# Moving GpSimd's side jobs around the state recurrences of a two-layer kernel

## The chip, the cores and the metric

The program runs on one core of one Trainium2 chip. Its time is the device time of one execution in microseconds (us). Each version is run several times on the same chip and the median is given. TensorE is PE in the rows, VectorE is DVE, ScalarE is ACT, GpSimd is POOL, and SP is the engine that issues most of the DMAs.

## The reference

Two pre-norm layers work on x, of 2 batches x 1024 rows x 128 features. The first has attention with 16 heads and a routed feed-forward part. The second has a selective state-space mixer and a dense mixture of eight experts. The change touches only the second layer:

```python
# mixer, for each batch; d_inner 256, d_state 16
h   = x @ fc1_w.T + fc1_b
...
hstate = dA * hstate + (dt_t * u_t)[..., None] * B_t[:, None, :]   # for each of 1024 steps
y_t    = jnp.einsum('bdn,bn->bd', hstate, C_t)
...
out = y @ out_proj_w.T
x   = x + out @ fc2_w.T + fc2_b
# dense experts, E = 8, hidden 256 each: every row goes through all of them
h = gelu(einsum('nd,edh->neh', xf, w1) + b1)
y = einsum('neh,ehd->ned', h, w2) + b2
x = x + (y * norm_g[:, None, None]).sum(axis=1)
```

## The kernel before

One Python list of steps, `K.order`, is walked once per engine. Each engine has a table from step names to functions (`POOL_STEPS` for GpSimd) and issues the instructions of those steps that it has, in the order of the list. So the place of a step in the list is its place in each engine's queue, and the queues run in order: an instruction that waits on a semaphore holds back all that stand behind it on its engine. `first_inputs_order`, `recurrence_order` and `dense_order` write the three parts of the list that matter here.

**Recurrences.** There are 2 batches x 2 halves of d_inner x 16 states = 64 units, `("unit", u)`, each over 1024 time steps. For each unit TensorE spreads a row of B over the partitions (L936), ScalarE forms the decay dA (L1387), VectorE multiplies the gain (L1923) and runs the scan (L1930), GpSimd multiplies the states by C (`hc`, L2252), and TensorE adds that product to Y (L952). The states and products have three buffers each. The dictionary `one` says which other steps stand behind which unit. Among them is `("fc2bias", b)`: GpSimd adds the bias fc2_b to batch b of x in place (L2230), once the normalised rows have been made from x. VectorE needs it later, in `dve_fc2`.

**Dense experts.** Full precision is got from three reduced-precision matmuls: high x high, high x low, low x high. ScalarE casts the weights to the high part (`w1hi`, `w2hi`), and GpSimd subtracts it from the weights to get the low part: `w1lo` e (L2260) and `w2lo` e (L2267), a 128x256 piece for each of the eight experts. TensorE's up products (`up1`, L1029) need `w1lo`; its down products (`down1`, L1046) need `w2lo`. There are 4 x 16 of each, numbered n; number n of the first 16 belongs to expert n // 2. The first 14 up products run behind units 49 to 62 and ScalarE parks their results (`pre`). ScalarE's gelu follows, its cast of the hidden part to high (L1471) and VectorE's subtraction for the low (`split1`, L2028: `e_hr_lo<-e_h,e_hr_hi`). Those hidden parts have four buffers. Down product n - 3 stands at step n of the dense list.

Two waits matter. The down products wait so:

```python
    if n < M1 and m % (F1 // P) == 0:
        pe.wait_ge(Y.w2_split, m // (F1 // P) + 1)
```

And `pre` number 11 overwrites the first layer's weight buffer that holds w1, so ScalarE first waits there until all eight `w1lo` are done (`Y.w1_split`, 8).

Beside the down products, the dense list has the layer norm of the second batch and the gate of the first. At step 11 stands `("lnvar", 7), ("lnroot", 7)`: VectorE's moments, then GpSimd's root (L2102, L2105). At step 12 stands `("e1_lg", 0), ("e1_root", 0)`: VectorE's gate sums (their last instruction L1960), then GpSimd's root of them (L2151).

Of the kernel before, what the change touches and what calls it, by code (L numbers as in the profile page):

```python
# [43 lines left out]
E1, F1 = 8, 256  # L44
# [17 lines left out]

PRE_EW = 11

LAST_ROWS, LAST_BANK = (B - 1, SEQ // CH - 1), B * (SEQ // CH) * M1 - 1


# [125 lines left out]
def turned(n):  # L193

    return [("lnturn", n, 0), ("lnturn", n, 1), ("lncopy", n, 0), ("lncopy", n, 1)]
# [158 lines left out]
def first_inputs_order():  # L354


    s = NSLOT
    order = turned(4) + [("down", s + 4), ("fc1", 0), ("fc1_out", 0), ("yrow", s + 4), ("fetch", s + 10)]
    order += [("down", s + 5), ("up", s + 6), ("gelu", s + 6), ("inp", 0, 0), ("inp_out", 0, 0), ("yrow", s + 5), ("fetch", s + 11)]
    order += [("inp", 0, 1), ("inp_out", 0, 1), ("up", s + 7), ("gelu", s + 7), ("down", s + 6)]  # L360
    for i in range(4):
        order += [("conv", 0, i // 2, w) for w in (i % 2 * 2, i % 2 * 2 + 1)]
        order += [("yrow", s + 6 + i)] + [("fetch", s + 12 + i)] * (i < 3) + ([("up", s + 8 + i), ("gelu", s + 8 + i), ("down", s + 7 + i)] if i < 3 else [])
    order += [("silu", 0, 0), ("up", s + 11), ("down", s + 10), ("silu", 0, 1), ("up", s + 12), ("yrow", s + 10)]
    order += [("xpj", 0), ("xpj_take", 0), ("gelu", s + 11), ("gelu", s + 12), ("pick",), ("up", s + 13), ("up", s + 14), ("dtp", 0, 0), ("xpj_out", 0)]
    order += [("gelu", s + 13), ("gelu", s + 14), ("xdr", 0), ("dtp_out", 0, 0), ("softexp", 0, 0), ("down", s + 11), ("yrow", s + 11), ("dtp", 0, 1), ("dtp_max",)]
    for n in range(s + 12, s + 15):
        order += [("down", n), ("yrow", n)]
    return order + [("softlog", 0, 0)]


def recurrence_order():

    beside = {u: [] for u in range(RECS + 1)}
    for t in range(NT):
        beside[t] += [("back", 1, t)]
        beside[t + 2] += [("rescale", t)]
    one = {0: [("expo", 1), ("softexp", 0, 1), ("softlog", 0, 1), ("first_skip",)], 1: [("rate", 1)], 2: [("inp", 0, 2)], 3: [("inp_out", 0, 2), ("inp", 0, 3)], 4: [("inp_out", 0, 3)], 5: [("e1_load",), ("wturn",), ("readd", 0)],
           6: [("wscale",), ("readd_out", 0), ("means", 0), ("centre", 0)], 7: [("squares", 0), ("halfroot", 0), ("wback", 0), ("wback", 1)],
           8: [("wback_out", 0), ("wback_out", 1), ("halfrows", 0)], 9: [("lnturn", 5, 0), ("lncopy", 5, 0), ("dt", 0, 1)],  # L380
           10: [("fc1", 1, 0), ("fc1_out", 1, 0), ("readd", 1), ("readd_out", 1), ("means", 1), ("centre", 1)],
           11: [("mix", 0, 0, 0), ("squares", 1), ("halfroot", 1)], 12: [("mix", 0, 1, 0), ("mix", 0, 2, 0), ("halfrows", 1), ("du", 0, 1)],
           13: [("mix", 0, 3, 0)], 14: [("lnturn", 5, 1), ("lncopy", 5, 1)], 15: [("fc1", 1, 1), ("fc1_out", 1, 1)],
           16: [("mix", 1, 0, 0), ("mix", 1, 1, 0)], 17: [("leave", 0, 0), ("gated", 0, 0), ("mix", 1, 2, 0), ("mix", 1, 3, 0)],
           18: [("silu", 1, 0, 0), ("silu", 1, 1, 0)], 19: [("mix", 0, 0, 1), ("mix", 0, 1, 1)], 20: [("mix", 0, 2, 1)],
           21: [("mix", 0, 3, 1), ("mix", 1, 0, 1), ("fc2bias", 0)], 22: [("mix", 1, 1, 1)], 23: [("mix", 1, 2, 1), ("mix", 1, 3, 1)],
           24: [("silu", 1, 0, 1), ("silu", 1, 1, 1), ("xpj", 1, 0)], XDR_UNIT: [("xpj", 1, 1), ("xpj_out", 1), ("xdr", 1)],
           26: [("dtp", 1, 0), ("dtp_out", 1, 0)], 27: [("softexp", 1, 0)], 28: [("softlog", 1, 0), ("dt", 1, 0)], 29: [("du", 1, 0)],
           33: [("leave", 0, 1), ("gated", 0, 1)], 35: [("outp", 0, 0)], 36: [("outp_out", 0, 0), ("outp", 0, 1)], 37: [("outp_out", 0, 1), ("fc2", 0, 0)],
           38: [("fc2", 0, 1), ("fc2_out", 0, 0)], 39: [("fc2_out", 0, 1)], 40: [("lnvar", 6), ("lnroot", 6), ("dtp", 1, 1)],  # L390
           41: [("dtp_out", 1, 1), ("lnrows", 6)], 43: turned(6)[:2] + [("softexp", 1, 1), ("softlog", 1, 1), ("fc2bias", 1)],
           44: turned(6)[2:] + [("dt", 1, 1), ("inp", 1, 2)], 45: [("inp_out", 1, 2), ("du", 1, 1)], 46: [("inp", 1, 3)],
           47: [("inp_out", 1, 3), ("w1hi", 0), ("w1lo", 0), ("xhi", 0, 0), ("xlo", 0, 0)], 55: [("xhi", 0, 1), ("xlo", 0, 1)]}
    for e in range(E1):
        one[48 + e - 1] = one.get(48 + e - 1, []) + [("w1hi", e), ("w1lo", e)] * (e > 0)
        one[56 + e] = [("w2hi", e), ("w2lo", e)]
    for i in range(EARLY_UPS):
        one[49 + i] += [("up1", i)]
        one[50 + i] += [("pre", i)]
    order = [("after", "inputs"), ("gain0",), ("dt", 0, 0), ("du", 0, 0), ("decay", 0), ("dtp_out", 0, 1)]  # L400
    for u in range(RECS + 1):
        if u == RECS:
            order.append(("after", "state"))
            order += [("up1", EARLY_UPS), ("up1", EARLY_UPS + 1)] + dense_step(0) + dense_step(1)
        order.append(("unit", u))
        order += beside[u] + one.get(u, [])
    return order


def dense_step(n):  # L410

    return [("gelu1", n)] + [("hi1", n)] * (n < EARLY_UPS) + [("split1", n)]


def dense_order():

    ahead = {4: [("output", 1, 1)], 7: [("outp_out", 1, 0)], 8: [("outp_out", 1, 1)], 9: [("fc2_out", 1, 0)], 10: [("fc2_out", 1, 1)],
             11: [("lnvar", 7), ("lnroot", 7)], 12: [("e1_lg", 0), ("e1_root", 0)], 13: [("lnrows", 7)], 15: [("e1_norm", 0)],
             17: [("e1_exp", 0)], 18: turned(7)[2:], 19: [("e1_top", 0)], 21: [("xhi", 1, 0)], 22: [("xhi", 1, 1)],
             23: [("xlo", 1, 0), ("e1_lg", 1), ("e1_root", 1)], 24: [("xlo", 1, 1)], 25: [("e1_norm", 1)], 31: [("e1_exp", 1)], 33: [("e1_top", 1)]}  # L420
    side = {2: [("b2s",)], 6: [("outp", 1, 0)], 7: [("outp", 1, 1)], 8: [("fc2", 1, 0)], 9: [("fc2", 1, 1)], 10: [("e1_gate", 0)],
            17: turned(7)[:2], 20: [("e1_gate", 1)]}
    order = []
    behind = {}
    for n in range(2, len(DENSE) + LAG + 2):
        order += ahead.get(n, []) + [("up1", EARLY_UPS + 2 + n // 4)] * (n in (2, 4))
        if EARLY_UPS < n < len(DENSE) - 3:
            order.append(("up1", n + 3))
        if n < len(DENSE):
            order += dense_step(n)  # L430
        order += side.get(n, [])
        if LAG <= n < len(DENSE) + LAG:
            b, c, m = DENSE[n - LAG]
            order.append(("down1", n - LAG))
            if m == M1 - 1:
                order.append(("sum1", b, c))
                behind[n + 1] = [("turn1", b, c), ("added", b, c)]
        order += behind.get(n, [])
    return order


def whole_order():
    return attention_order() + routed_order() + first_inputs_order() + recurrence_order() + dense_order()
# [2253 lines left out]
```

## Time and profile before

| | |
|---|---|
| median of 3 runs | 1121.9 us (1121.43 to 1122.65) |
| the profiled execution | 1121.12 us, of which the span 1119.8 us |
| TensorE matmul busy | 1066.3 us, 95% |
| VectorE busy | 839.1 us, 75% |
| ScalarE busy | 630.4 us, 56% |
| GpSimd busy | 763.4 us, 68% |
| mean granted clock of TensorE | 0.991 of full speed |

The rows further down come from this one execution. Times in them count from the span's start. The recurrences fill about 790 to 1021 us and the dense experts the rest, with their early up products inside the recurrences. A share of busy time over the whole span says little about either, since it mixes them with the attention of the first 690 us.

### The profile page before, as it was taken

Reading aid. Unit: us, or ns where it says so; the run is one execution under the profiler, and the core shown is the slowest. Engines: PE = TensorE matmul, PEld = TensorE weight load, DVE = VectorE, ACT = ScalarE, POOL = GpSimd, SP = SyncE. Lnnn points to the kernel's source line nnn. Section 1 sums busy time; section 2 is a strip of 40 time slices with the busy share of each in tenths; the row PEclk is TensorE's granted clock in tenths of the full one; section 3 lists DMA queues with packets and bytes.
Section 4 is the critical chain, followed back from the end, with each engine's and each line's share of the span. In section 5 each row is a group of like instructions: output and inputs, shape, how many; then the busy total and the mean of one; then the engine's idle time right before and its main releaser. Section 6 shows DMA issues by size and latency. Waiting matters only on the chain.

```text
span 1119.8 us, 18526 instructions
## 1 busy us (share of the span) xinstructions
PE 1066.3 (95%) x6860; PEld 662.1 (59%) x6860; DVE 839.1 (75%) x1234; ACT 630.4 (56%) x898; POOL 763.4 (68%) x394
## 2 busy tenths in 40 slices
PE   7999999999999999999999999779789987999998
PEld 4555665665665655665665657767344433446786
DVE  6876976776765775766975748235999999997987
ACT  5554655654644654643554635348986646757663
POOL 5788788787787897877899830230789897994200
PEclk9999999999999999999999999889899999999999
DMA  7000000000000000000000253465565443440000
GB/s 213 1 2 2 1 2 1 2 2 1 2 2 2 1 1 2 2 2 1 6 7 6 77 178 94 136 215 151 182 206 165 143 161 132 147 154 20 10 10 19
DMA packets 55369, 68.91 MB, mean 62 GB/s; under 512 B 23248, under 2 KB 41424, under 8 KB 55280
## 3 DMA queue, kind: packets, MB, share of 16 engines
q1 hardware_dynamic: 52272, 64.65, 18.7%
q0 software_dynamic: 1024, 2.10, 0.6%
q8 instruction: 55, 0.90, 0.3%
q10 hardware_dynamic: 1984, 0.98, 0.3%
q14 instruction: 34, 0.28, 0.1%
HBM read 61.30 MB, written 6.16 MB: 60 GB/s over the span
## 4 chain that ended last, share of the span: by engine, by line
PE 79%; issue 7%; DVE 6%; POOL 4%; ACT 3%; DMA 1%; another core or an unknown queue 1%; POOLq 0%; DVEq 0%; ACTq 0%
PE psum L661 20%; PE psum L622 16%; PE psum L647 6%; PE psum L635 5%; PE psum L1046 3%; PE psum L687 3%; PE psum L952 3%; PE psum L1029 3%; POOL hc L2252 3%; PE psum L746 3%; PE psum L702 2%; PE psum L810 2%; PE psum L821 2%; PE psum L726 2%; PE psum L680 2%
## 5 line engine op out<-in xcount | busy, mean ns | idle before, releaser
L2164 POOL TENSOR_TENSOR psums<-psums,prob 128x1024 f32<-128x1024 f32 x180 | 430.5, 2392 | 26.1 <-POOL psums L2164 0.5
L1627 DVE TENSOR_REDUCE mx<-psum 128x2 f32<-128x1024 f32 x256 | 299.8, 1218 | 102.0 <-PE psum L647 101.6
L1158 ACT ACTIVATE prob<-psum 128x1024 f32<-128x1024 f32 x256 | 261.3, 1026 | 62.6 <-PE psum L635 38.1
L661 PE MATMUL psum<-prob,V 128*64 128x512 f32 x1024 | 238.7, 597 | 0.0
L2252 POOL TENSOR_TENSOR hc<-hs,cc 128x1024 f32<-128x1024 f32 x64 | 151.6, 2368 | 21.1 <-DVE hs L1930 18.6
L1930 DVE TENSOR_TENSOR_SCAN hs<-dA,psum 128x1024 f32<-128x1024 f32 x64 | 146.3, 2287 | 2.2
L661 PEld LDWEIGHTS psum<-prob,V 128*64 128x64 f32 x1024 | 67.7, 137 | 106.7 <-issue 105.0
L2164 POOL TENSOR_TENSOR psums<-prob 128x1024 f32<-128x1024 f32 x30 | 72.1, 2403 | 85.0 <-ACT prob L1158 84.2
L1177 ACT COPY oraw<-psum 128x512 f32<-128x512 f32 x32 | 18.8, 587 | 191.3 <-PE psum L661 191.3
L952 PE MATMUL psum<-hc,ident 128*128 128x512 f32 x256 | 122.5, 601 | 2.8 <-DVE slot_rows_h L1938 1.4
L647 PE MATMUL psum<-k_hi,q_hi 64*128 64x512 f32 x512 | 107.0, 409 | 1.7 <-DVE mx L1627 1.3
L622 PE MATMUL psum<-q_hi,k_hi 64*128 64x512 f32 x512 | 106.2, 403 | 0.0
L622 PE MATMUL psum<-q_hi,k_lo 64*128 64x512 f32 x512 | 103.0, 390 | 0.0
L622 PE MATMUL psum<-q_lo,k_hi 64*128 64x512 f32 x512 | 103.0, 390 | 0.0
L635 PE MATMUL psum<-guard,row_one 64*128 64x512 f32 x512 | 102.4, 388 | 0.0
L1692 DVE SCALAR_TENSOR_TENSOR x<-psum,inv,x 128x128 f32<-128x128 f32 x256 | 72.1, 345 | 23.5 <-PE psum L746 21.9
L952 PEld LDWEIGHTS psum<-hc,ident 128*128 128x128 f32 x256 | 48.1, 191 | 44.6 <-issue 32.2
L647 PEld LDWEIGHTS psum<-k_hi,q_hi 64*128 64x128 f32 x512 | 49.8, 184 | 41.1 <-issue 28.4
L936 PE MATMUL psum<-xdr,pickr 128*128 128x512 f32 x128 | 55.8, 517 | 18.0 <-DVE hs L1930 17.8
L622 PEld LDWEIGHTS psum<-q_hi,k_hi 64*128 64x128 f32 x512 | 48.7, 184 | 32.5 <-ACT prob L1158 16.9
L1387 ACT ACTIVATE dA<-slotT,alog 128x1024 f32<-128x1024 f32 x32 | 36.6, 1150 | 40.1 <-DVE hs L1930 39.7
L635 PEld LDWEIGHTS psum<-guard,row_one 64*128 64x128 f32 x512 | 50.3, 184 | 9.0
(319 smaller groups left out, 1712.6 us busy)
## 6 DMA issues: line engine op xcount, KB each, us to landing
cc<-C_rows SPq DMA_DIRECT2D x64, 512.0 KB, 3.8
kq_wts<-in_e_rows SPq DMA_DIRECT2D x14, 578.0 KB, 4.2
e_wts<-in_e_rows SPq DMA_DIRECT2D x10, 578.0 KB, 3.9
e_w<-in_e_rows SPq DMA_DIRECT2D x6, 578.0 KB, 5.1
slots_in<-e_zero SPq DMA_DIRECT2D x2, 960.0 KB, 7.1
inv<-sum_rows SPq DMA_DIRECT2D x120, 1.0 KB, 2.0
slots_out<-e_y SPq DMA_DIRECT2D x30, 64.0 KB, 1.8
e_w<-in_e_w SPq DMA_DIRECT2D x1, 1024.0 KB, 7.0
```

The source lines that it names most:

```text
L622: pe.matmul(both[:, s, :], left[HALF[s], js], right[HALF[s], cs], start=(part == 0), stop=False)
L635: ins = pe.matmul(both[:, s, :], A.row_one[HALF[s], :], A.guard[q][HALF[s], cs], start=False, stop=True)
L647: ins = pe.matmul(both[:, s, :], A.q_hi[r][HALF[s], t * P:(t + 1) * P], A.k_hi[r][HALF[s], c * CH:(c + 1) * CH], start=True, stop=True)
L661: ins = pe.matmul(A.O[HALF[s], :], A.V[pair % 2][:, j, s * DH:(s + 1) * DH], A.prob[unit(pair, c, j) % NPB][:, s * CH:(s + 1) * CH], start ...
L936: ins = pe.matmul(X.gain[u % 2][:, c * CH:(c + 1) * CH], X.pickr[:, n:n + 1].broadcast_to([P, P]), X.xdr[b][:, c * CH:(c + 1) * CH], start ...
L952: ins = pe.matmul(X.Y[:, c * CH:(c + 1) * CH], K.ident[:, :], X.hc[u % 3][:, c * CH:(c + 1) * CH], start=(u > 0 and n == 0), stop=(n == NS ...
L1158: act.activation(A.prob[n % NPB][:, :], slots.bank("score", pair, c, j).rearrange("p s n -> p (s n)"), ACT.Exp, scale=float(DH) ** -0.5).t ...
L1627: dve.tensor_reduce(K.A.mx[:, :, t, c], slots.bank("max", pair, t, c), AXX, ALU.max).then_inc(*slots.inc("max", pair, t, c))
L1692: ins = dve.scalar_tensor_tensor(out=K.x[:, tile, :], in0=slots.bank("out", pair, c)[:, s, t * P:(t + 1) * P], scalar=A.inv[:, inv_column( ...
L1930: dve.tensor_tensor_scan(X.hs[u % 3][:, :], X.dA[u % 3][:, :], X.gain[u % 2], 0.0, ALU.mult, ALU.add).then_inc(X.state_done, 1)
L2164: pool.tensor_tensor(total[:, :], (K.A.prob[(n - 1) % NPB] if j == 1 else total)[:, :], K.A.prob[n % NPB][:, :], ALU.add).then_inc(*K.psum ...
L2252: pool.tensor_tensor(X.hc[u % 3][:, :], X.hs[u % 3][:, :], X.cc[u % NCC][:, :], ALU.mult).then_inc(X.product_done, 1)
```

## The change

Three sets of GpSimd's steps get other places in the list; no instruction is added or removed, and the queues of the other engines keep their order. The bias addition of the first batch goes from behind unit 21 to ahead of the recurrences. `w1lo` 1 to 7 go from behind units 48 to 54 to behind units 48, 50, ..., 60. `w2lo` 0 to 7 go from behind units 56 to 63 to steps 2, 4, ..., 16 of the dense list.

```diff
+W1_LOW = {e: 46 + 2 * e for e in range(1, E1)}
...
-    order = turned(4) + [("down", s + 4), ("fc1", 0), ("fc1_out", 0), ("yrow", s + 4), ("fetch", s + 10)]
+    order = turned(4) + [("down", s + 4), ("fc1", 0), ("fc1_out", 0), ("fc2bias", 0), ("yrow", s + 4), ("fetch", s + 10)]
...
-           21: [("mix", 0, 3, 1), ("mix", 1, 0, 1), ("fc2bias", 0)], 22: [("mix", 1, 1, 1)], 23: [("mix", 1, 2, 1), ("mix", 1, 3, 1)],
+           21: [("mix", 0, 3, 1), ("mix", 1, 0, 1)], 22: [("mix", 1, 1, 1)], 23: [("mix", 1, 2, 1), ("mix", 1, 3, 1)],
...
     for e in range(E1):
-        one[48 + e - 1] = one.get(48 + e - 1, []) + [("w1hi", e), ("w1lo", e)] * (e > 0)
-        one[56 + e] = [("w2hi", e), ("w2lo", e)]
+        one[48 + e - 1] = one.get(48 + e - 1, []) + [("w1hi", e)] * (e > 0)
+        one[56 + e] = [("w2hi", e)]
+    for e in range(1, E1):
+        one[W1_LOW[e]] += [("w1lo", e)]
...
         order += ahead.get(n, []) + [("up1", EARLY_UPS + 2 + n // 4)] * (n in (2, 4))
+        order += [("w2lo", n // 2 - 1)] * (n % 2 == 0 and n // 2 <= E1)
```

In GpSimd's queue the end of the recurrences and the dense part read so before. `hc` is the product of states and C, `e1_w2_lo` a piece of `w2lo`, `std` and `rstd` the layer norm's root, `e1_s1` the gate's root; in brackets are the semaphores that an instruction waits for.

```order
L2252 TENSOR_TENSOR hc1<-hs1,cc1 128x1024 [waits added,product_done,C_spread1,state_done]
L2267 TENSOR_TENSOR e1_w2_lo<-e1_w,e1_w2_hi 128x256 [waits w_hi,w2_split]
L2252 TENSOR_TENSOR hc2<-hs2,cc2 128x1024 [waits added,product_done,C_spread2,state_done]
L2267 TENSOR_TENSOR e1_w2_lo<-e1_w,e1_w2_hi 128x256 [waits w_hi,w2_split]
L2252 TENSOR_TENSOR hc0<-hs0,cc3 128x1024 [waits added,product_done,C_spread3,state_done]
L2267 TENSOR_TENSOR e1_w2_lo<-e1_w,e1_w2_hi 128x256 [waits w_hi,w2_split]
L2102 TENSOR_SCALAR std<-mv 128x8 [waits ln_variance]
L2105 TENSOR_TENSOR rstd<-std,exponent 128x8 [waits pool_own]
L2151 TENSOR_TENSOR e1_s1<-e1_s1,exponent 128x8 [waits ms_done] x2
```

And now (four lines were added above, so L2256 is the old L2252, L2271 the old L2267, and so on):

```order
L2256 TENSOR_TENSOR hc1<-hs1,cc1 128x1024 [waits added,product_done,C_spread1,state_done]
L2256 TENSOR_TENSOR hc2<-hs2,cc2 128x1024 [waits added,product_done,C_spread2,state_done]
L2256 TENSOR_TENSOR hc0<-hs0,cc3 128x1024 [waits added,product_done,C_spread3,state_done]
L2271 TENSOR_TENSOR e1_w2_lo<-e1_w,e1_w2_hi 128x256 [waits w_hi,w1_split]
L2271 TENSOR_TENSOR e1_w2_lo<-e1_w,e1_w2_hi 128x256 [waits w_hi,w2_split] x4
L2106 TENSOR_SCALAR std<-mv 128x8 [waits ln_variance]
L2109 TENSOR_TENSOR rstd<-std,exponent 128x8 [waits pool_own]
L2155 TENSOR_TENSOR e1_s1<-e1_s1,exponent 128x8 [waits ms_done]
L2271 TENSOR_TENSOR e1_w2_lo<-e1_w,e1_w2_hi 128x256 [waits w_hi,w2_split] x3
L2155 TENSOR_TENSOR e1_s1<-e1_s1,exponent 128x8 [waits ms_done]
```

All eight pieces of `w2lo` left the units; five of them now stand directly behind the last product, and the last three (experts 5 to 7) behind the second batch's layer norm root and the first batch's gate root.

Ahead of the recurrences, GpSimd's queue read so before; `du` is the first thing that it does for the units:

```order
L2102 TENSOR_SCALAR std<-mv 128x8
L2105 TENSOR_TENSOR rstd<-std,exponent 128x8
L2215 TENSOR_TENSOR du<-dt,u 128x1024
L2252 TENSOR_TENSOR hc<-hs,cc 128x1024
```

And now:

```order
L2106 TENSOR_SCALAR std<-mv 128x8
L2109 TENSOR_TENSOR rstd<-std,exponent 128x8
L2234 TENSOR_TENSOR x<-x,fc2b 128x1024
L2219 TENSOR_TENSOR du<-dt,u 128x1024
L2256 TENSOR_TENSOR hc<-hs,cc 128x1024
```

The bias addition of the first batch stands between the layer norm's root and `du`.

## Rows read from the trace of the kernel before

**Rows 1.** The page: busy us (share of the span) and instructions of each engine.
```profile
PE 1066.3 (95%) x6860; PEld 662.1 (59%) x6860; DVE 839.1 (75%) x1234; ACT 630.4 (56%) x898; POOL 763.4 (68%) x394
```

**Rows 2.** The page: groups; line, engine, op, count, busy and mean ns, idle before.
```profile
L2252 POOL TENSOR_TENSOR hc<-hs,cc 128x1024 f32<-128x1024 f32 x64 | 151.6, 2368 | 21.1 <-DVE hs L1930 18.6
L1930 DVE TENSOR_TENSOR_SCAN hs<-dA,psum 128x1024 f32<-128x1024 f32 x64 | 146.3, 2287 | 2.2
```

**Rows 3.** All waits of VectorE, 795 to 1018 us: total us, times, longest.
```profile
DVE psum L1923 <- PE psum L936: 3.2, 6, 0.9
```

**Rows 4.** Timeline, SP and GpSimd: start, us, engine; ahead of and within the units.
```profile
724.00 0.45 SPq L2381 DMA_DIRECT2D e_rms<-in_e_rms  x1
...
750.57 1.67 POOL L2105 TENSOR_TENSOR rstd<-std,exponent 128x8 f32<-128x8 f32 x1
789.20 2.35 POOL L2215 TENSOR_TENSOR du<-dt,u 128x1024 f32<-128x1024 f32 x1 [36.95 <-DVE dt L1891]
...
886.43 2.35 POOL L2200 TENSOR_TENSOR xdr<-xd,xdr 64x1024 fp32r<-64x1024 f32 x1 [1.78 <-ACT xdr L1334]
```

**Rows 5.** Timeline of GpSimd: end of the units, dense part.
```profile
1011.01 0.74 POOL L2267 TENSOR_TENSOR e_w_lo<-e_w,e_w_hi 128x256 fp32r<-128x256 f32 x1
...
1019.02 2.36 POOL L2252 TENSOR_TENSOR hc<-hs,cc 128x1024 f32<-128x1024 f32 x1 [0.38 <-DVE hs L1930]
1021.34 1.20 POOL L2267 TENSOR_TENSOR e_w_lo<-e_w,e_w_hi 128x256 fp32r<-128x256 f32 x1
1038.72 0.59 POOL L2102 TENSOR_SCALAR std<-mv 128x8 f32<-128x8 f32 x1 [16.18 <-DVE mv L1549]
1039.39 1.74 POOL L2105 TENSOR_TENSOR rstd<-std,exponent 128x8 f32<-128x8 f32 x1
1041.10 1.63 POOL L2151 TENSOR_TENSOR e_s<-e_s,exponent 128x8 f32<-128x8 f32 x1
```

**Rows 6.** Timeline of ScalarE: `pre` numbers 11 and 12.
```profile
1009.99 0.58 ACT L1464 COPY e_w<-psum 128x512 f32<-128x512 f32 x1
...
1013.56 0.59 ACT L1464 COPY e_w<-psum 128x512 f32<-128x512 f32 x1 [2.69 <-PE psum L1029]
```

**Rows 7.** Line L2028: duration ns min/median/max, first and last start us.
```profile
L2028 DVE TENSOR_TENSOR e_hr_lo<-e_h,e_hr_hi x64: 657/693/2126, 1019.8 to 1114.0; 128x512 fp32r<-128x512 f32 x64
```

**Rows 8.** Timeline of TensorE: down products 0, 10, 11, then three with idle before.
```profile
1023.96 0.40 PE L1046 MATMUL psum<-e_hr_hi,e_w_hi 128*128 128x512 f32 x1
...
1038.62 0.39 PE L1046 MATMUL psum<-e_hr_hi,e_w_hi 128*128 128x512 f32 x1
...
1039.31 0.44 PE L1046 MATMUL psum<-e_hr_hi,e_w_hi 128*128 128x512 f32 x1
...
1041.29 0.50 PE L1029 MATMUL psum<-e_x_hi,e_w_hi 128*128 128x512 f32 x1 [1.06 <-ACT e_h L1453]
...
1043.97 0.51 PE L1046 MATMUL psum<-e_hr_hi,e_w_hi 128*128 128x512 f32 x1 [0.32 <-DVE e_hr_lo L2028]
...
1048.23 0.50 PE L1029 MATMUL psum<-e_x_hi,e_w_hi 128*128 128x512 f32 x1 [1.02 <-ACT e_h L1453]
```

**Rows 9.** Timeline of VectorE: the gate sums' end, and split number 13.
```profile
1039.89 0.17 DVE L1960 TENSOR_SCALAR e_s<-e_s 128x8 f32<-128x8 f32 x1
...
1043.23 0.68 DVE L2028 TENSOR_TENSOR e_hr_lo<-e_h,e_hr_hi 128x512 fp32r<-128x512 f32 x1
```

**Rows 10.** Busy us (count) by stretch: PE, PEld, DVE, ACT, POOL; then TensorE's granted clock.
```profile
719.20:722.80 3.60, 0.00 (x0) 0.00 (x0) 0.58 (x2) 1.11 (x5) 0.81 (x1) 0.80 0.29 66
722.80:728.10 5.30, 5.22 (x24) 5.22 (x25) 0.29 (x1) 2.19 (x9) 0.00 (x0) 0.50 0.61 164
743.30:748.80 5.50, 0.00 (x0) 0.00 (x0) 3.06 (x12) 1.14 (x5) 2.03 (x3) 0.68 0.57 164
748.80:752.20 3.40, 3.35 (x16) 3.35 (x17) 1.57 (x12) 1.41 (x5) 1.87 (x2) 0.52 0.88 259
1050.00:1116.00 66.00, 65.74 (x298) 53.24 (x297) 56.50 (x124) 35.06 (x54) 1.96 (x1) 1.00 0.04 13
```

## The prediction

> **What bounds the kernel now.** I read the page's busy shares first, then its costliest groups, then the waits of the engine that looks full in the units, and last the timelines at the places from which and to which steps move. The page calls TensorE 95% busy [rows 1], but that mixes stages, so each stage has to be read by itself.
>
> In the units, 64 products on GpSimd take 2.37 us each and 64 scans on VectorE 2.29 us [rows 2]. VectorE also multiplies the gain for each unit, GpSimd has the side jobs. Which is the bound? GpSimd sat idle 18.6 us before its products because it waited for the scan [rows 2]; the other way round there is nothing: between 795 and 1018 us VectorE waited 3.2 us in all, each time for TensorE's spread of B, and never for GpSimd [rows 3]. So VectorE sets the pace of the units. GpSimd is a follower with slack, even if it runs some units late for a while and catches up.
>
> In the dense part TensorE sets the pace: between 1050 and 1116 us it was busy 65.74 of 66.00 us [rows 10]. Its 298 matmuls there give 66.00/298 = 0.22 us each with the small ones among them; down product 10 starts at 1038.62 and number 11 at 1039.31 [rows 8], so one up or down product of three matmuls takes 0.69 us, say 0.7. Before 1050 it has three waits, and these are all the slack there is: 1.06, 0.32 and 1.02 us [rows 8]. The last down products sit against the end of the kernel, so time lost on TensorE's queue beyond this slack is lost for good.
>
> **The bias addition of the first batch.** An addition of 128x1024 on GpSimd takes 2.35 us, as `du` of the same shape does [rows 4]. Its new place is a hole: the layer norm's root starts at 750.57 and takes 1.67 us, and the next thing, `du`, starts at 789.20 after 36.95 us of idle time, released by VectorE [rows 4]. It waits for the last of the small loads, whose last issue is at 724.00 [rows 4], and for the normalised rows, some us after the root. It hides in the hole; cost 0, and if the load came late 30 us of cover would have to go first. What its old place gives back: GpSimd has caught up again by 886.43, where it waits 1.78 us for ScalarE [rows 4], and VectorE never waited for it. I take 0. Bounds: nothing lost; at most what VectorE waited for TensorE behind it, which is a part of the 3.2 us [rows 3]. I put that part at 0.9 us, the longest single wait of these; the far end of 3.2 stays in the rival below.
>
> **w1lo later.** Seven pieces, of 0.74 us if they take what a piece of w2lo of the same shape does [rows 5], move back by up to 6 units. TensorE's up products follow behind unit 49 + n and need piece n // 2, which now stands behind unit 46 + n; to be at its place TensorE must have added a product that GpSimd issued later than that piece. No wait for TensorE. ScalarE has one: `pre` number 11 waits for all eight. The eighth now follows the product of unit 60, where the piece at 1011.01 stood in the old order, so it ends at 1011.75 [rows 5]; `pre` 11 started at 1009.99 [rows 6]. It slips by 1.8 us. Behind it on ScalarE stand a short cast and `pre` 12, which began at 1013.56 after 2.69 us of waiting for TensorE [rows 6]. The slip fits in there: 0.
>
> **w2lo off the units.** Eight pieces leave. The last product starts at 1019.02 after waiting 0.38 us for the scan [rows 5], not for a piece, so it does not move: 0 gained.
>
> **w2lo 0 to 4 behind the last product.** GpSimd is free from 1021.38. One piece took 0.74 us alone, but the one at 1021.34 took 1.20 [rows 5], and VectorE's `e_hr_lo`, 0.69 us in the median, took 2.13 us once, its first being at 1019.8 [rows 7], inside the product of 1019.02. Both read two SBUF tensors. The rows say that while GpSimd's instruction holds on, VectorE's waits, and the other way round. With 1.2 us for each piece, the five end at 1022.6, 1023.8, 1025.0, 1026.2, 1027.4. Down product 0 starts at 1023.96 [rows 8]: 1.4 us to spare, and the later ones need one piece for two products. VectorE's splits 2 to 4 slip by up to 0.6 us each, about 1 us in sum. I take 0 for TensorE, with 0 and 1 us as ends: it still has other products between these.
>
> The Trainium skill (SBUF — State Buffer, section "Who interferes with whom") says that a VectorE instruction with two SBUF inputs contends with a GpSimd instruction that reads SBUF, and that the second one blocks until the first is done. The trace agrees with its 2.13 and 1.20 us [rows 5, 7]; by the rule every piece moved behind the recurrences collides with a split, by the median alone none would.
>
> **w2lo 5 to 7: the step that decides.** GpSimd's queue now has the layer norm root and the gate root ahead of piece 5. They wait for VectorE: the moments release `std` at 1038.72, `rstd` starts at 1039.39, the gate root at 1041.10 and takes 1.63 us, though its input was ready at 1039.89 + 0.17 = 1040.06 [rows 5, 9]. So GpSimd is free for piece 5 at 1042.73. The piece takes 0.74 to 1.20 us, and VectorE's split 13 at 1043.23 [rows 9] may cross it: done at 1043.5 to 1043.9; I take 1043.65 with the semaphore. Down product 10 is the first that needs it (expert 10 // 2 = 5), and its turn is at 1038.62 [rows 8]. Before, the piece was long done. TensorE stands still for 1043.65 - 1038.62 = 5.0 us, and behind the waiting matmul all else is queued: down 11, up 18, down 12 and so on, none of which could pass. The engines that feed it gain little in that time: only four hidden buffers exist, so split 14 needs down 10 done.
>
> How much comes back: TensorE's later waits vanish, since what it waited for is there by then. That is 1.06 + 0.32 + 1.02 = 2.40 us [rows 8], and three times 0.27 us, because a wait is counted from the modelled end of a matmul of 0.39 to 0.50 us while its successor follows after 0.23: 0.8. Together 3.2. Left over: 5.0 - 3.2 = 1.8 us. Pieces 6 and 7 follow within 2.4 us, before down 12 (2.1 us after down 10) or shortly at it, and down 14 much later: 0, at most 0.3.
>
> **The clock.** Where TensorE did nothing for the 3.6 us from 719.20 the granted clock was 0.80 in the mean, and then 0.50, the 1.2 GHz level, for the next 5.3 us of full work; after 5.5 us of nothing at 743.30 (mean 0.68) it was 0.52 for 3.4 us [rows 10]. An idle stretch of 5.0 us lies between these two, so I expect the clock to be at 1.2 GHz when down 10 starts and to stay there for 3.4 to 5.3 us of work. Half of that is lost: 1.7 to 2.65 us; I take 2.0, nearer the idle stretch of 5.5 us. It finds no slack, as that is used up.
>
> **Sum.** 0 + 0 + 0 + 0 + 1.8 + 2.0 = +3.8 us. On the profiled execution: 1121.12 + 3.8 = 1124.9 (span 1119.8 + 3.8 = 1123.6 and 1.3 around it). The median before is 0.8 above that execution, so 1121.9 + 3.8 = 1125.7 us.
>
> **Rivals.**
> - *The stall comes, the clock stays.* Then only 1.8 us (up to 2.2 with a piece of 1.20 us): 1123.7. For it: the two idle stretches in the rows are only two. Against: both, one shorter and one longer than this, ended at 0.50.
> - *No stall.* Piece 5 would have to be done by 1038.6, so the two roots would have to run 5 us sooner than in the rows, or the piece to go ahead of them. The order rows speak against it; then all edits are hidden: 1121.9.
> - *The relief reaches VectorE: not slower.* The mechanism is in the units behind the old place of the bias addition and from unit 49 on: products come up to 2.35 us and 0.74 us sooner, TensorE adds them sooner and spreads the next B sooner, and VectorE's waits for L936 shrink. Price: up to 0.9 us of the 3.2 [rows 3], plus 0.5 us where the split of 1019.8 no longer meets a piece: 1121.9 - 1.4 = 1120.5. All 3.2 would give 1118.7. It decides only if there is no stall at down 10; with the stall it shortens the loss at most to 2.4.
> - *The stall grows.* The about 1 us that VectorE loses beside pieces 0 to 4 delays its moments and the roots, so piece 5 too, and the clock takes 2.65: 1121.9 + 1.8 + 1.0 + 2.65 + 0.3 = 1127.7.
>
> **How the numbers follow.** Forecast (stall and low clock) 0.68; clock stays 0.10; no stall 0.09; relief 0.06; grown stall 0.07. The forecast alone spans 1.4 + 1.7 = 3.1 to 2.3 + 2.65 = 4.95 us, so 1125.0 to 1126.9. For 8 in 10 I reach down into the case of the clock that stays and up into the grown stall: 1123.4 to 1127.4. A measurement here tells about 0.2% (2.2 us) from no change, so slower is above 1124.1: 0.68 + 0.07 and a little of the second case, 0.76. Within: the rest of that case, no stall and most of the relief, 0.18. Faster: 0.06.
>
> **What would show it.** Right: in the timeline after, TensorE idle for about 5 us before a down product, released by GpSimd's `e_w_lo` of L2271; this piece directly behind the gate root; granted clock near 0.5 for the next 3 to 5 us; the three waits of 0.32 to 1.06 us gone; VectorE's scans at the same times as before to a few tenths; GpSimd's gaps in the units wider. The bias addition at about 755 us with idle time on both sides. Wrong: if no idle over 1 us stands before a down product, the sum is 0 and its main step false; if the last scan ends over 1 us earlier, GpSimd did hold VectorE back; if the clock is at 1.00 right after the stall, the term of 2.0 goes.

## The result and the profile after

| | median | profiled execution | its span |
|---|---|---|---|
| before (7 runs) | 1122.24 us (1120.44 to 1123.84) | 1121.12 us | 1119.8 us |
| changed (7 runs) | 1125.65 us (1124.58 to 1127.26) | 1124.58 us | 1123.3 us |

The changed kernel takes 1.003 times as long, 95% interval 1.0018 to 1.0042: slower by 3.4 us (2.0 to 4.7). The forecast was +3.8 us, 1125.7 us.

First GpSimd's timeline, end of the units and dense part (start us, us, engine, line, tiles, count, and the idle time before with what ended it). It answers to [rows 5].

```profile
1010.53 0.74 POOL L2264 TENSOR_TENSOR e_w_lo<-e_w,e_w_hi 128x256 fp32r<-128x256 f32 x1
...
1018.54 2.36 POOL L2256 TENSOR_TENSOR hc<-hs,cc 128x1024 f32<-128x1024 f32 x1 [1.08 <-DVE hs L1934]
1020.87 5.46 POOL L2271 TENSOR_TENSOR e_w_lo<-e_w,e_w_hi 128x256 fp32r<-128x256 f32 x5
1038.24 0.59 POOL L2106 TENSOR_SCALAR std<-mv 128x8 f32<-128x8 f32 x1 [11.92 <-DVE mv L1553]
1038.91 1.73 POOL L2109 TENSOR_TENSOR rstd<-std,exponent 128x8 f32<-128x8 f32 x1
1040.62 1.63 POOL L2155 TENSOR_TENSOR e_s<-e_s,exponent 128x8 f32<-128x8 f32 x1
1042.22 3.14 POOL L2271 TENSOR_TENSOR e_w_lo<-e_w,e_w_hi 128x256 fp32r<-128x256 f32 x3
```

Five pieces of `w2lo` follow the last product, and GpSimd then sits idle for 11.92 us with three pieces still to do, because the two roots stand ahead of them. The roots here are 0.48 us earlier than in [rows 5], since this execution reached the last scan that much sooner (1016.18 us against 1016.66).

TensorE's timeline, which answers to [rows 8]: down products 9, 10 and 11, up 18, and up 21.

```profile
1037.44 0.40 PE L1050 MATMUL psum<-e_hr_hi,e_w_hi 128*128 128x512 f32 x1
...
1043.07 0.79 PE L1050 MATMUL psum<-e_hr_hi,e_w_hi 128*128 128x512 f32 x1 [4.76 <-POOL e_w_lo L2271]
...
1044.51 0.63 PE L1050 MATMUL psum<-e_hr_hi,e_w_hi 128*128 128x512 f32 x1
...
1045.79 0.63 PE L1033 MATMUL psum<-e_x_hi,e_w_hi 128*128 128x512 f32 x1
...
1051.99 0.40 PE L1033 MATMUL psum<-e_x_hi,e_w_hi 128*128 128x512 f32 x1
```

The stall is 4.76 us, and what ended it (its releaser) is the piece on GpSimd. After it a product of three matmuls takes 1.28 us (1044.51 to 1045.79) instead of 0.7. The page's busy shares of the two kernels cannot show this: TensorE is "95% busy" in both.

Busy time by stretch (PE, PEld, DVE, ACT, POOL, then the granted clock), as in [rows 10]:

```profile
1038.30:1043.00 4.70, 0.01 (x1) 0.00 (x0) 4.10 (x13) 4.65 (x7) 4.62 (x4) 0.84 0.00 0
1043.00:1048.40 5.40, 5.33 (x13) 4.18 (x14) 4.38 (x11) 1.27 (x3) 2.21 (x3) 0.50 0.00 0
1053.80:1120.00 66.20, 65.64 (x299) 53.18 (x298) 55.83 (x123) 35.48 (x55) 1.96 (x1) 1.00 0.04 13
```

For 5.4 us of full work the clock was at its 1.2 GHz level: half of that, 2.7 us at the most, is lost. The mean of 0.84 in the stall says that the clock had fallen to that level for the last 1.5 us of it (0.16 x 4.70 / 0.50). The other waits of TensorE in the dense part, from the answer on all its waits (total us, times, longest), before and after:

```profile
PE psum L1029 <- ACT e_h L1453: 2.1, 2, 1.1
PE psum L1046 <- DVE e_hr_lo L2028: 0.3, 1, 0.3
```

```profile
PE psum L1050 <- POOL e_w_lo L2271: 4.8, 1, 4.8
```

The three old waits are gone, one new one is there. (Both kernels also have one of 0.6 us at the end, for ScalarE, and some of up to 0.3 us inside the recurrences.)

The units, answering to [rows 2] and [rows 3]:

```profile
L2256 POOL TENSOR_TENSOR hc<-hs,cc 128x1024 f32<-128x1024 f32 x64 | 151.8, 2371 | 28.0 <-DVE hs L1934 25.5
```

```profile
DVE psum L1927 <- PE psum L940: 3.5, 6, 1.2
```

GpSimd now waits 25.5 us for the scans instead of 18.6; VectorE waits 3.5 us for TensorE instead of 3.2. The relief went into GpSimd's own idle time.

**How small differences are read below.** The first scan begins between 782.3 and 790.7 us in the ten profiles of this study, as the stages ahead of it vary from one execution to the next. From the first scan to the last they differ by up to 1.6 us. That spread is found again in VectorE's waits for TensorE's spread of B, which were 3.2 to 5.1 us in the ten: 3.5 to 4.8 in the five kernels with the bias addition moved, 3.2 to 5.1 in the five without. What makes these waits vary is open; the place of the bias addition does not. The time from the last scan's start to the end of the span, called the tail here, varies less: it is 103.14 us before (1119.8 - 1016.66) and 107.12 after (1123.3 - 1016.18), +3.98 us. Kernels whose dense parts take the same course agreed within 0.15 us, though each tail is that of one profiled execution.

Medians and their intervals are given beside it. Experiments 1 to 4 and 5 to 8 were two later rounds on two different chips, where the kernel before, run again in each, took 1118.04 and 1121.59 us in the median; each ratio is to those runs, and only tails are compared across rounds.

### The profile page after: what moved, and what is told of

It reads as the page before. It is cut to its first block, busy times and chain, and to the rows that moved or that the text cites. A ratio compares the mean times of both kernels' runs of the same rounds, so it can differ in the third digit from the quotient of the medians.

```text
span 1123.3 us, 18526 instructions
## 1 busy us (share of the span) xinstructions
PE 1068.1 (95%) x6860; PEld 665.3 (59%) x6860; DVE 841.6 (75%) x1234; ACT 631.0 (56%) x898; POOL 766.2 (68%) x394
## 4 chain that ended last, share of the span: by engine, by line
PE 80%; DVE 7%; issue 6%; POOL 3%; ACT 2%; DMA 1%; another core or an unknown queue 1%; SPq 0%; POOLq 0%; DVEq 0%; ACTq 0%
PE psum L665 20%; PE psum L626 16%; PE psum L651 6%; PE psum L639 5%; PE psum L1050 4%; PE psum L691 3%; DVE psum L1927 3%; PE psum L1033 3%; PE psum L956 3%; PE psum L750 3%; PE psum L706 2%; PE psum L814 2%; PE psum L825 2%; POOL hc L2256 2%; PE psum L730 2%
## 5 line engine op out<-in xcount | busy, mean ns | idle before, releaser
L2256 POOL TENSOR_TENSOR hc<-hs,cc 128x1024 f32<-128x1024 f32 x64 | 151.8, 2371 | 28.0 <-DVE hs L1934 25.5
```

The source lines that it names most:

```text
L2256: pool.tensor_tensor(X.hc[u % 3][:, :], X.hs[u % 3][:, :], X.cc[u % NCC][:, :], ALU.mult).then_inc(X.product_done, 1)
```

## The experiments

**1. All pieces ahead of the roots.** Is it the roots that hold the pieces back?

```diff
-        order += [("w2lo", n // 2 - 1)] * (n % 2 == 0 and n // 2 <= E1)
+        order += [("w2lo", n - 2)] * (n - 2 < E1)
```

> The changed kernel, but all eight w2lo pieces stand at steps 2 to 9 of the dense list, ahead of the layer norm root and the gate root; the bias addition and w1lo stay at their new places. Theory (the loss is the stall of down product 10 behind the two roots): no idle time of TensorE over 1.3 us between 1023 and 1050 us, span and median back at those of the kernel before, so about 3.4 us below the changed kernel. Rival (the loss comes from pieces that collide with VectorE's splits, or from the moved steps in the units): eight pieces collide instead of five, the time stays at +3 us or more over before.

Measured: ratio to before 0.9999 (0.9987 to 1.0011), tail 103.06 us. GpSimd's queue in it:

```profile
1014.43 8.89 POOL L2271 TENSOR_TENSOR e_w_lo<-e_w,e_w_hi 128x256 fp32r<-128x256 f32 x8
1031.80 0.59 POOL L2106 TENSOR_SCALAR std<-mv 128x8 f32<-128x8 f32 x1 [8.48 <-DVE mv L1553]
```

Eight pieces at 1.11 us each beside VectorE's splits, and TensorE's old waits are back unchanged. So the bias addition, `w1lo` and the collisions cost nothing together that can be told (0.08 us less in the tail, 1.5 us less to 1.2 more in the medians); the place behind the roots costs all.

**2. Only the last three pieces late.**

```diff
-        one[56 + e] = [("w2hi", e), ("w2lo", e)]
+        one[56 + e] = [("w2hi", e)] + [("w2lo", e)] * (e < 5)
...
+        order += [("w2lo", n // 2 - 1)] * (n in (12, 14, 16))
```

> The kernel before, with nothing moved but w2lo 5 to 7, which go to steps 12, 14 and 16 of the dense list as in the changed kernel. Theory: these three carry the whole loss: stall of 4.8 us before down product 10, +3.4 us over before (2.5 to 4.5). Rival (bias addition, w1lo or the first five pieces carry a part): clearly less than the changed kernel's +3.4, under 2.

Measured: ratio 1.0047 (1.0033 to 1.0061), tail 107.26 us, +4.12. The median's difference of 5.3 us (3.7 to 6.8) is above the expected range's end, the tail within it; its interval and the changed kernel's 2.0 to 4.7 overlap, and the tails differ by 0.14 us. Why the medians lie further apart than the tails is open. Three steps of 0.7 to 1.2 us on GpSimd, moved, make the whole loss.

```profile
1041.84 0.79 PE L1047 MATMUL psum<-e_hr_hi,e_w_hi 128*128 128x512 f32 x1 [4.68 <-POOL e_w_lo L2268]
```

**3. The stall filled with work.** What do stall and clock cost apart?

```diff
+def pe_fill(K, pe):
+    for _ in range(FILL):    # 20
+        pe.matmul(K.work.banks[7], K.Y.w2s[0][:, 0, :], K.Y.hr[2][0][:, :], start=True, stop=True)
...
+    pe.wait_ge(Y.h_split, n + 1)
+    if n == 10:
+        pe_fill(K, pe)
     if n < M1 and m % (F1 // P) == 0:
         pe.wait_ge(Y.w2_split, m // (F1 // P) + 1)
-    pe.wait_ge(Y.h_split, n + 1)
```

The down products' wait for the hidden part goes ahead of their wait for the piece, because the added matmuls read that hidden part.

> The changed kernel, plus 20 matmuls of 512 columns into an unused PSUM bank ahead of down product 10 (results unused), which take 20 x 0.23 = 4.7 us in the time that TensorE otherwise stands idle. Theory of two terms (stall less slack 1.7 to 1.8 us, lowered clock about 2.3 us): the granted clock stays at 1.00, and the time is 2.0 to 2.6 us below the changed kernel, +1.2 to 1.9 over before. Rival (the clock costs nothing here, since other engines bound the stretch): same as the changed kernel within 0.5 us.

Measured: ratio 1.0016 (1.0007 to 1.0025), +1.8 us; tail 104.73, +1.59 over before and 2.39 under the changed kernel.

```profile
1034.40:1039.30 4.90, 4.88 (x21) 3.56 (x20) 4.30 (x15) 4.82 (x8) 4.64 (x4) 1.00 0.00 0
1039.30:1044.30 5.00, 4.98 (x22) 4.01 (x23) 4.83 (x12) 1.17 (x3) 1.95 (x2) 1.00 0.00 0
```

The columns are those above. TensorE is late all the same, but at full clock: 22 matmuls in 5.0 us against 13 in 5.4. Down product 10 started as long after the last scan as in the changed kernel (26.85 us against 26.89), so what differs behind it is the clock. The stall less its slack costs 1.6 us and the clock 2.4. The split rests on the tails: by the medians the filled kernel is 1.6 us nearer to before than the changed one, and 3.5 nearer than `last_three` of its own round. The rival, by which the clock is free, falls.

**4. One piece ahead of the gate root.** How much slack is there, and does a shorter stall keep the clock?

```diff
-             ... 12: [("e1_lg", 0), ("e1_root", 0)], ...
+             ... 12: [("e1_lg", 0)], ...
         order += [("w2lo", n // 2 - 1)] * (n % 2 == 0 and n // 2 <= E1)
+        order += [("e1_root", 0)] * (n == 12)
```

> The changed kernel with one swap in GpSimd's queue: the gate root (1.63 us) behind w2lo piece 5 instead of ahead of it. The piece starts at about 1040.6 instead of 1042.2, so TensorE's idle time before down product 10 is 3.1 to 3.4 us instead of 4.8. Theory (3.2 us of slack come back): if the clock stays, the time equals before within 0.5 us; if it falls all the same, +2.0 to 2.6 over before. Rival (each us of stall costs a us, no slack): +2.4 us less than the 4.8 would, i.e. 1.6 us below the changed kernel and no more.

Measured: ratio 1.0015 (1.0006 to 1.0024), +1.7 us; tail 104.63, +1.49. TensorE's wait, and the stretches around it:

```profile
1039.86 0.50 PE L1051 MATMUL psum<-e_hr_hi,e_w_hi 128*128 128x512 f32 x1 [3.08 <-POOL e_w_lo L2272]
```

```profile
1037.00:1039.80 2.80, 0.00 (x0) 0.00 (x0) 2.20 (x7) 2.77 (x6) 2.72 (x4) 1.00 0.00 0
1039.80:1043.60 3.80, 3.74 (x10) 2.98 (x11) 3.77 (x11) 1.87 (x3) 3.72 (x4) 0.59 0.00 0
1043.60:1048.00 4.40, 4.40 (x24) 3.63 (x24) 3.96 (x10) 2.71 (x5) 0.17 (x1) 0.97 0.00 0
```

The stall of 3.08 us fits into the slack of 3.2 us; what is left is the clock. Means of 0.59 over 3.80 us and 0.97 over 4.40 us are a loss of 0.41 x 3.80 + 0.03 x 4.40 = 1.7 us, and 1.49 were measured. The whole loss, 1.49 us, is well below the stall of 3.08, which no stall without slack could give: the rival falls. (The tail fell by 2.5 us for 1.7 us of stall, but part of that is the clock, whose low stretch was shorter too.) The case in which the clock falls had been priced at +2.0 to 2.6 us; the tail's 1.49 lies below it, the median's 1.7 (0.7 to 2.7) reaches into it.

**5. The bias addition alone.**

```diff
-           21: [("mix", 0, 3, 1), ("mix", 1, 0, 1), ("fc2bias", 0)], ...
+           21: [("mix", 0, 3, 1), ("mix", 1, 0, 1)], ...      # and in first_inputs_order as in the change
```

> The kernel before with one step moved: the first batch's bias addition ahead of the recurrences, as in the changed kernel. Theory (GpSimd has slack in the units, VectorE never waits for it): same as before within 0.2%; from the start of the first scan to that of the last 226.2 us plus what one execution differs from the next (up to 1.5 us so far); TensorE's waits in the dense part unchanged. Rival (relief reaches VectorE): up to 0.9 us less between first and last scan and in the time.

Measured: ratio 1.0006 (0.9996 to 1.0017), tail 103.06, first to last scan 227.48 us. No gain, and no cost that can be told: the interval leaves room for 0.5 us less and 1.9 us more, and TensorE's waits in the dense part are those of before. From first to last scan 1.3 us more is within the spread told above (`last_three`, with the addition at its old place, took 227.40). The addition runs in the hole:

```profile
754.24 2.36 POOL L2230 TENSOR_TENSOR x<-x,fc2b 128x1024 f32<-128x1024 f32 x1 [2.32 <-DVE xrows L1587]
788.27 2.35 POOL L2215 TENSOR_TENSOR du<-dt,u 128x1024 f32<-128x1024 f32 x1 [31.67 <-DVE dt L1891]
```

**6 to 8. Can the slack itself be turned into time?** The kernel before, with steps of the dense list one place later: rows and exponential; the gate's matmuls; all three.

```diff
-   13: [("lnrows", 7)], ... 17: [("e1_exp", 0)], 18: turned(7)[2:]     # exp_rows
+   14: [("lnrows", 7)], ... 18: [("e1_exp", 0)] + turned(7)[2:]
-   side = {... 10: [("e1_gate", 0)],                                   # gate_only
+   side = {... 11: [("e1_gate", 0)],
```

> The kernel before with two steps of the dense list one place later, w2lo as before: the second batch's rows (lnrows 7, 2.15 us of VectorE) at step 14 instead of 13, behind split 13; the first batch's gate exponential (ScalarE, which waited 2.23 us for its input) at step 18 instead of 17, behind gelu 17. Theory (TensorE sets the pace of the dense part and its three waits are all the slack): the waits of 0.32 and 1.02 us go, from the last scan's start to the end 101.5 to 101.9 us instead of 103.1, time 1.2 to 1.6 us below before. Rival (VectorE is as full as TensorE from 1041 to 1063 us): the waits return some steps later, gain under 0.5 us.

> The kernel before with one step moved: the first batch's gate matmuls (16 of 8 columns, 1.7 us of TensorE) at step 11 instead of 10, so behind down product 7, whose hidden buffer ScalarE waits for (1.24 us). Theory: the wait of 1.06 us before up product 18 goes, gain up to 1.3 us if the later two waits don't grow by it, none if they do (both hang on VectorE's queue and the gate's chain, which do not move). I expect 0 to -0.5 us: 102.6 to 103.1 us from the last scan's start to the end.

> Both edits together: rows at step 14, exponential at step 18, gate matmuls at step 11. Theory: all three waits go, 3.2 us of slack turn into time: 100.0 to 100.8 us from the last scan's start to the end, time 2.3 to 3.1 us below before. Rival (VectorE becomes the bound): 0.5 to 1.5 us below before, with TensorE waiting for VectorE's splits between 1040 and 1060 us.

Measured:

| kernel | ratio to before | tail us | TensorE's waits |
|---|---|---|---|
| exp_rows | 0.9994 (0.9984 to 1.0004) | 102.15 | 1.06, 0.77 |
| gate_only | 1.0011 (1.0001 to 1.0020) | 103.08 | 0.48, 0.88, 1.02 |
| exp_rows_gate | 0.9990 (0.9981 to 0.9999) | 101.98 | 0.47, 1.17 |

The two kernels with the exponential moved gained less than expected: 1.0 us in the tail instead of 1.2 to 1.6, and 1.2 instead of 2.3 to 3.1. `gate_only` has the tail that was expected (102.6 to 103.1), but a median 0.1% above before's instead of below. Where the old wait went is seen with all three edits, in ScalarE's timeline:

```profile
1044.16 1.28 ACT L1417 ACT_TABLE_LOAD   x1
1047.09 0.26 ACT L1417 ACTIVATE e_lg<-e_lg 128x64 f32<-128x64 f32 x1 [1.64 <-DVE e_lg L1973]
1047.25 1.06 ACT L1107 COPY xnT<-psum 128x512 f32<-128x512 f32 x2
1048.33 1.28 ACT L1453 ACT_TABLE_LOAD   x1
1049.62 0.69 ACT L1453 ACTIVATE e_h<-psum,e_b 128x512 f32<-128x512 f32 x1
```

In the kernel before, the same place read:

```profile
1046.19 1.28 ACT L1453 ACT_TABLE_LOAD   x1
1047.48 0.69 ACT L1453 ACTIVATE e_h<-psum,e_b 128x512 f32<-128x512 f32 x1
1048.07 1.07 ACT L1107 COPY xnT<-psum 128x512 f32<-128x512 f32 x2
```

The exponential still waits for VectorE and has a table load before and after it, 5.5 us without a gelu in all; TensorE runs dry one up product later than before. My expectation had this block cost TensorE nothing once gelu 17 was ahead of it. It also overlooked two copies (`xnT`, 1.06 us together): they belong to step 18, so they now follow the exponential directly and hold back the gelu that TensorE waits for, where before a gelu stood between. With the copies behind that gelu it would start about 1.06 us sooner and leave 0.1 of TensorE's wait of 1.17 us. That is an estimate from these rows; no run tried it. So these three runs do not show how much of the slack could be had.

The rival of the last kernel, VectorE as the bound, has the right size (0.5 to 1.5 us below before), but what it said of the waits did not come: TensorE waited for ScalarE's gelu, not for VectorE's splits. Moving the gate only moved TensorE's waits: 2.38 us of them against 2.40 before. The last kernel has the shortest tail, 1.2 us below before's and 0.2 below that of `exp_rows`; in the medians it is 0.1% (0.01 to 0.19%) below before. `gate_only` is as far above before (0.01 to 0.20%) with an unchanged tail, so neither is more than the edge of what was measured.

## Why the prediction was right, point by point

- **VectorE sets the pace of the units; relief of GpSimd gives 0.** Held: experiments 1 and 5, and GpSimd's idle time that grew by 6.9 us for nothing. The 3.2 us of VectorE's waits that bounded the relief were those of one execution; others had up to 5.1. The 0.5 us that the rival gave a split freed of a piece were misread: that split, at 1019.81 us, ran beside the product of 1019.02 and had been going 1.5 us when the piece began, and in the changed kernel it took 2.11 us instead of 2.13.
- **`w1lo` later: `pre` 11 slips by 1.8 us into slack.** Held. ScalarE's timeline of the changed kernel: it waited 1.75 us, and `pre` 12 still waited for TensorE.

```profile
1011.35 0.59 ACT L1468 COPY e_w<-psum 128x512 f32<-128x512 f32 x1 [1.75 <-POOL e_w_lo L2264]
...
1013.08 0.59 ACT L1468 COPY e_w<-psum 128x512 f32<-128x512 f32 x1 [0.84 <-PE psum L1033]
```

- **Pieces 0 to 4: 1.2 us each, 0 for TensorE.** Held: 5.46 / 5 = 1.09 us each, no wait of TensorE.
- **The stall.** Forecast 5.0 us, from GpSimd free at 1042.73 and the piece done at 1043.65; measured 4.76 between records and 4.93 between the starts (1043.07 against 1038.62 - 0.48). Right in mechanism, place and size. Piece 5 took 0.79 us and did not meet split 13.
- **The slack, 3.2 us of it.** Held: left over 1.8 us forecast, 1.59 measured with the clock held up (experiment 3), so 4.93 - 1.59 = 3.3 us of slack. The 0.27 us beside each wait is right in size, but only 0.17 of it is the modelled end (0.40 less 0.23 us); the other 0.10 is the first matmul behind a wait, whose successor follows after 0.33 us (1041.29 to 1041.62).
- **The clock.** Right in kind, the term under-sized: 2.0 us forecast, 2.39 measured (107.12 - 104.73; with the tail of `last_three` it is 2.53), inside the stated 1.7 to 2.65. I had taken the value of the longer idle stretch of the two in [rows 10]; the 5.4 us at the low level are those of the shorter one. The length of a stall does not give it: idle stretches of 3.6, 4.76, 5.5 and 3.08 us were followed by 5.3, 5.4, 3.4 and 3.4 us of work at the low level. In the first three, what differs is how much of the low time was over before the work began again: by the means 0.80, 0.84 and 0.68 it was 1.4, 1.5 and 3.5 us, and low clock in idle time costs nothing. Experiment 4 had none of it in the idle time and still only 3.4 us behind; why stays open.
- **The sum.** +3.8 forecast; +3.98 in the tail, +3.4 (2.0 to 4.7) in the medians. That the sum came so near is in part luck: the stall's rest was 0.2 us too large and the clock's term 0.4 too small. The rival "no stall" falls with the 4.76 us in the trace, "relief" with experiments 1 and 5, "the clock stays" with the stretches at 0.50. "The stall grows" is also out: the moments released `std` at 1038.24 + 0.48 = 1038.72, the same time as before. The forecast's bounds of 1.4 and 2.3 us for the stall less its slack have no working; its own terms give 1.7 to 2.4.

Two more kinds of VectorE's instructions were slowed that the prediction had not weighed. The eight `tensor_scalar` of the second batch's rows took 2.67 us instead of 2.15 beside a piece, and a cast 0.90 us where 0.42 is the median:

```profile
1040.68 2.67 DVE L1591 TENSOR_SCALAR xrows<-x,mv,rstd 128x128 f32<-128x128 f32 x8 [0.50 <-POOL rstd L2109]
...
1044.75 0.90 DVE L2030 CAST e_hr_hi<-e_h 128x512 fp32r<-128x512 f32 x1 [0.80 <-PE psum L1050]
```

The Trainium skill (SBUF — State Buffer, section "Who interferes with whom") says that `cast` and `tensor_scalar` can run in two-port modes and then contend with GpSimd, if their operands meet the conditions of such a mode. The trace agrees: both were slowed beside a piece, to 2.67 and 0.90 us. Both ran while TensorE was behind anyway, and no later wait of TensorE is seen.

## What to carry to other kernels

Before a step is moved in an in-order queue, ask what stands ahead of it at the new place and when that is released: here 0.7 us of work was put behind two small roots that wait for another engine, and became a stall of 4.8 us although the engine had 12 idle us just before. Relief of an engine that only follows another was worth nothing here; the first question is who ever waits for it. A stall of TensorE in a stretch that it bounds had two prices: its length less the waits that vanish behind it (1.6 us), and the low clock after it (2.4 us). The stall had used up the slack, so the clock found none.

## What the runs showed of the hardware

- The clock can fall after work has begun again. In experiment 4 it was at 1.00 through the whole idle time, and TensorE resumed at 1039.86; then it fell to the 1.2 GHz level while TensorE was busy. Two stretches of 1 us of that kernel, columns as above, show where it fell and rose; between them it was at 0.50, 3.4 us in all:

```profile
1040.00:1041.00 1.00, 1.00 (x4) 0.82 (x5) 1.00 (x5) 0.98 (x2) 1.00 (x1) 0.73 0.00 0
1043.00:1044.00 1.00, 1.00 (x4) 0.81 (x3) 0.97 (x2) 0.00 (x0) 0.77 (x1) 0.56 0.00 0
```

  So the clock at the end of a stall does not tell what the work behind it gets.
- Useless work in a stall was worth 2.4 us in the tail. In experiment 3 the twenty matmuls end just when the piece is done, and down product 10 starts right behind them:

```profile
1034.45 4.83 PE L1043 MATMUL psum<-e_hr_hi,e_w_hi 128*128 128x512 f32 x20
1039.32 0.50 PE L1060 MATMUL psum<-e_hr_hi,e_w_hi 128*128 128x512 f32 x1
```
